# Scores by single key tiles in three PSUM banks, a fourth ring bank, and tiled products kept together

## What is computed

```python
q = _heads(h @ wq); k, v = _heads(ctx @ wk), _heads(ctx @ wv)
sim = jnp.einsum('bhnd,bhmd->bhnm', q, k) * dh ** -0.5
a = jax.nn.softmax(sim, axis=-1)                    # over 256 or 1601 keys
o = jnp.einsum('bhnm,bhmd->bhnd', a, v)
x = x + o_merged @ wo + bo
```

## Time and profile before

| | |
|---|---|
| median of 3 runs | 7120.51 us (7119.77 to 7120.83) |
| profiled execution | 7129.41 us, span 7127.6 us |
| mean granted TensorE clock | 0.956 |
| TensorE busy | 6424.0 us, 90% |
| VectorE busy | 4929.0 us, 69% |
| ScalarE busy | 3981.7 us, 56% |
| GpSimd busy | 2707.1 us, 38% |

### The profile page before, as it was taken

The page is one execution under the profiler, slowest core; times in us unless marked ns, Lnnn a source line. Parts: engine busy times, 40 slices in busy tenths (PEclk is TensorE's granted clock), DMA queues, the critical chain, the costliest instruction groups (busy, mean ns, idle before and its releaser), DMA issues.

```text
span 7127.6 us, 119830 instructions
## 1 busy us (share of the span) xinstructions
PE 6424.0 (90%) x43254; PEld 3725.9 (52%) x43254; DVE 4929.0 (69%) x9886; ACT 3981.7 (56%) x7106; POOL 2707.1 (38%) x2326
## 2 busy tenths in 40 slices
PE   6899889989889998998988999899897999989988
PEld 4555445653455544565455554556444555346644
DVE  6777666657777766665777776666577776766656
ACT  4454565655545557565654555756474445565656
POOL 2446114651144611565014551156401455116630
PEclk9999999999999999999999999999999999999999
DMA  3101011100111001111011100111001010011100
GB/s 81 33 25 26 22 27 32 28 27 18 44 32 27 25 21 31 29 30 29 12 46 31 29 24 20 33 28 30 26 16 46 25 30 24 18 35 28 29 18 11
DMA packets 347633, 204.00 MB, mean 29 GB/s; under 512 B 165006, under 2 KB 319982, under 8 KB 346927
## 3 DMA queue, kind: packets, MB, share of 16 engines
q1 hardware_dynamic: 347054, 196.34, 10.7%
HBM read 105.18 MB, written 1.05 MB: 15 GB/s over the span
## 4 chain that ended last, share of the span: by engine, by line
PE 68%; DVE 12%; ACT 9%; POOL 6%; issue 4%; SPq 1%; DVEq 0%; POOLq 0%; DMA 0%; ACTq 0%
PE ring L1309 34%; PE o_acc L1309 17%; PE scores L1309 16%; DVE max_part L2042 6%; POOL weight_sum L1271 4%; ACT qop L1593 4%; ACT probs L1719 2%; DVE region L2004 1%; DVE o_inv L2073 1%; DVE ring L2021 1%; ACT qm L1593 1%; ACT region L1593 1%; DVE ring L2018 1%; POOL qm L1290 1%; PE ring L1405 1%
## 5 line engine op out<-in xcount | busy, mean ns | idle before, releaser
L2042 DVE TENSOR_REDUCE max_part<-ring 128x1 f32<-128x400 f32 (+2 forms) x4608 | 2454.9, 578 | 829.4 <-PE ring L1309 813.8
L1719 ACT ACTIVATE probs<-scores 128x1024 f32<-128x1024 f32 (+1 forms) x2048 | 1917.6, 969 | 1231.0 <-PE scores L1309 845.3
L1271 POOL TENSOR_TENSOR weight_sum<-weight_sum,probs 128x512 f32<-128x512 f32 (+1 forms) x1408 | 1785.7, 1268 | 143.5 <-ACT probs L1719 2.4
L1309 PE MATMUL o_acc<-probs,region 128*32 128x256 f32 (+2 forms) x13312 | 1360.1, 389 | 0.0
L1271 POOL TENSOR_TENSOR weight_sum<-probs 128x512 f32<-128x512 f32 x256 | 324.8, 1269 | 2125.9 <-PE ring L1309 1794.1
L1593 ACT ACTIVATE region<-ring 64x400 f16<-64x400 f32 (+4 forms) x1744 | 815.0, 477 | 520.5 <-PE ring L1309 416.4
L1309 PEld LDWEIGHTS o_acc<-probs,region 128*32 128x32 f32 (+2 forms) x13312 | 589.0, 123 | 534.0 <-issue 317.9
L1593 ACT ACTIVATE qop<-ring 64x256 f16<-64x256 f32 (+1 forms) x1536 | 563.4, 375 | 446.9 <-DVE ring L2021 278.8
L1309 PE MATMUL scores<-qop,region 128*128 128x256 f16 (+1 forms) x3328 | 781.6, 275 | 12.6 <-ACT probs L1719 8.1
L1309 PE MATMUL ring<-nk,qm 128*128 128x400 f16 (+2 forms) x2560 | 720.6, 343 | 79.2 <-DVE max_part L2042 42.6
L1309 PE MATMUL scores<-qop,x_cop 128*128 128x256 f16 (+1 forms) x3328 | 778.0, 274 | 0.0
(11 more groups left out here) (159 smaller groups left out, 7449.6 us busy)
## 6 DMA issues: line engine op xcount, KB each, us to landing
x_cop<-region SPq DMA_DIRECT2D x256, 200.1 KB, 3.1
stage<-in_wide SPq DMA_DIRECT2D x512, 64.0 KB, 2.0
nk<-region SPq DMA_DIRECT2D x192, 100.1 KB, 2.2
stage<-in_wide SPq DMA_DIRECT2D x128, 128.0 KB, 2.6
v_stage<-in_wide SPq DMA_DIRECT2D x256, 64.0 KB, 1.8
wo_stage<-in_wide SPq DMA_DIRECT2D x32, 512.0 KB, 4.0
cop_few<-kop_few SPq DMA_DIRECT2D x256, 32.0 KB, 1.9
ff_w<-in_ff_w SPq DMA_DIRECT2D x24, 256.0 KB, 3.1
```

The costliest lines, as they stand in the source:

```text
L1271: pool.tensor_tensor(total, before, probs[0:rows_, g % PROBS, at:at + BANK], ALU.add)\
L1309: return pe.matmul(out, lhs, rhs, start=start, stop=stop, skip_group_check=True)
L1719: act.activation(to, src, ACT.Exp, scale=t.scale).then_inc(exp_done.sem, 1)
L2042: dve.tensor_reduce(dst, src, AX.X, ALU.max).then_inc(*release(one))
```

## The change

Scores, exponentials and probabilities go by single key tiles: a chunk is one tile, `scores` has three banks for three chunks, `probs` eight slots of half the size. The bank that this frees goes to the ring, now four. Value products, the GpSimd sums and the release of probability slots still go by pairs of tiles (`chunks_of`). The due times of the scores are spread evenly over a unit's time. The planner's `run` remembers whether TensorE's last part used column tiles (`in_tiles`: value products and `sum`); a part of the other kind counts as due `STAY = 1.0` later, and 0.1 longer. The planned costs of scores, exponentials and value products are restated. The diff without its context lines:

```diff
@@ -23,7 +23,9 @@
-RING, SLOTS, PROBS = 3, 2, 4
+RING, SLOTS, PROBS = 4, 3, 8
+STAY = 1.0
@@ -40,7 +42,7 @@
-        self.chunks = self.pairs * self.halves
+        self.chunks = self.kt * self.halves
@@ -89,6 +91,10 @@
+    def chunks_of(self, pair):
+        return range(2 * pair * self.halves, min(2 * pair + 2, self.kt) * self.halves)
@@ -236,8 +242,8 @@
-                half = prev.t.halves == 2 and prev.t.cross and cb % 2 == 0
-                at = values_at[prev.n, cb // prev.t.halves] - 0.001 - half * 0.5 * prev.t.time / prev.t.pairs
+                t = prev.t
+                at = values_at[prev.n, 0] - 0.001 + (cb / t.chunks) * t.time * (t.cross or 0.5)
@@ -246,8 +252,11 @@
+            at = max(at, done.get("scores", at) + 0.0001)
+            if c == 0:
+                scores_at[un.n] = at
...
-            scored[un.n] = at
+            scored[un.n] = done["scores"] = at
@@ -360,6 +369,11 @@
+def in_tiles(what):
+    return what[0] == "values" or what[0] == "job" and UNITS[what[1]].t.jobs[what[2]][0] == "sum"
@@ -381,9 +395,10 @@
-        out = [("PE", ("values", un.n, c // un.t.halves))]
+        pair = c // un.t.halves // 2
+        out = [("PE", ("values", un.n, pair))]
...
-            out.append(("POOL", ("values", un.n, c)))
+            out.append(("POOL", ("values", un.n, pair)))
@@ -567,7 +582,6 @@
-        pair = c // t.halves
@@ -575,18 +589,17 @@
-        tiles = len(t.tiles(pair))
-        self.part("PE", "scores", due, one, (0.45 if t.wide else 0.23) * tiles, deps, 0.2)
+        self.part("PE", "scores", due, one, 0.44 if t.wide else 0.22, deps, 0.2)
...
-        self.part("ACT", "exp", due, one, 1.02 if tiles == 2 else 0.6, deps)
+        self.part("ACT", "exp", due, one, 0.58, deps)
...
-        deps = [("ACT", ("scores", un.chunk + pair * t.halves + k)) for k in range(t.halves)]
+        deps = [("ACT", ("scores", un.chunk + c)) for c in t.chunks_of(pair)]
@@ -597,12 +610,11 @@
-        self.part("PE", "values", due, one, 0.53 * tiles, deps, 0.25)
+        self.part("PE", "values", due, one, 0.43 * tiles, deps, 0.25)
...
-            deps = [("ACT", ("scores", un.chunk + pair))]
...
-                deps.append(("PE", ("job", old.n, old.t.sum_job)))
+                deps = [*deps[:t.chunks_of(0)[-1] + 1], ("PE", ("job", old.n, old.t.sum_job))]
@@ -650,7 +662,7 @@
-        events, now, left = [], 0.0, len(self.parts)
+        events, now, left, tiled = [], 0.0, len(self.parts), False
@@ -660,6 +672,8 @@
+                    if e == "PE" and in_tiles(what) != tiled:
+                        due = due[0] + STAY, due[1]
@@ -672,6 +686,9 @@
+                if e == "PE":
+                    dur += 0.1 * (in_tiles(what) != tiled)
+                    tiled = in_tiles(what)
@@ -836,7 +853,7 @@
-        probs = sb("probs", [P, PROBS, 2 * BANK])
+        probs = sb("probs", [P, PROBS, BANK])
@@ -868,7 +885,7 @@
-        scores = psum("scores", [P, 2 * SLOTS, BANK])
+        scores = psum("scores", [P, SLOTS, BANK])
@@ -1252,8 +1269,7 @@
-                    g = un.chunk + pair
-                    pool.wait_ge(exp_done.sem, exp_done.at(n, pair + 1))
+                    pool.wait_ge(exp_done.sem, exp_done.at(n, t.chunks_of(pair)[-1] + 1))
@@ -1261,14 +1277,13 @@
-                        at = (k % 2) * BANK
...
-                        before = probs[0:rows_, g % PROBS, 0:BANK] if k == 1 else total
+                        before = probs[0:rows_, un.chunk % PROBS, :] if k == 1 else total
...
-                        pool.tensor_tensor(total, before, probs[0:rows_, g % PROBS, at:at + BANK], ALU.add)\
+                        pool.tensor_tensor(total, before, probs[0:rows_, (un.chunk + k) % PROBS, :], ALU.add)\
@@ -1516,7 +1531,7 @@
-                    pair, half = c // t.halves, c % t.halves
+                    k, half = c // t.halves, c % t.halves
@@ -1526,18 +1541,16 @@
-                    first = 2 * (g % SLOTS)
-                    for k in t.tiles(pair):
-                        r = t.rows(k)
-                        if t.wide:
-                            out = scores[0:r, first + k % 2, :]
-                            for h in range(2):
-                                mm(out[:, h * N:(h + 1) * N], kop_of(un)[:, h, k * P:k * P + r], qop[:, z, h, :], True, False)
-                                last = mm(out[:, h * N:(h + 1) * N], cop_of(un)[:, h, k * P:k * P + r], qop[:, z, 2 + h, :],
-                                          False, True)
-                        else:
-                            last = mm(scores[0:r, first + k % 2, :], nk[:, un.narrow_at % NK_SLOTS, k * P:k * P + r],
-                                      qm[:, un.narrow_at % QM_SLOTS, 2 * half:2 * half + 2, :], True, True)
+                    r = t.rows(k)
+                    out = scores[0:r, g % SLOTS, :]
+                    if t.wide:
+                        for h in range(2):
+                            mm(out[:, h * N:(h + 1) * N], kop_of(un)[:, h, k * P:k * P + r], qop[:, z, h, :], True, False)
+                            last = mm(out[:, h * N:(h + 1) * N], cop_of(un)[:, h, k * P:k * P + r], qop[:, z, 2 + h, :],
+                                      False, True)
+                    else:
+                        last = mm(out, nk[:, un.narrow_at % NK_SLOTS, k * P:k * P + r],
+                                  qm[:, un.narrow_at % QM_SLOTS, 2 * half:2 * half + 2, :], True, True)
@@ -1555,14 +1568,13 @@
-                    pe.wait_ge(exp_done.sem, exp_done.at(n, (pair + 1) * t.halves))
+                    pe.wait_ge(exp_done.sem, exp_done.at(n, t.chunks_of(pair)[-1] + 1))
...
-                        r, at = t.rows(k), k % 2
+                        r = t.rows(k)
...
-                            g = un.chunk + pair * t.halves + h // 2
-                            slot = g % PROBS
-                            w = probs[0:r, slot, at * BANK + (h % 2) * N:at * BANK + (h % 2 + 1) * N]
+                            g = un.chunk + k * t.halves + h // 2
+                            w = probs[0:r, g % PROBS, (h % 2) * N:(h % 2 + 1) * N]
@@ -1701,21 +1713,15 @@
-                    pair = c // t.halves
...
-                        act.wait_ge(av_done.sem, av_done.at(old.n, co // old.t.halves + 1))
+                        pair = co // old.t.halves // 2
+                        act.wait_ge(av_done.sem, av_done.at(old.n, pair + 1))
...
-                            act.wait_ge(weight_step.sem, weight_step.at(old.n, old.t.adds(co)))
-                    to = probs[:, g % PROBS, :].rearrange("p (k n) -> p k n", k=2)
-                    src = scores[:, 2 * (g % SLOTS):2 * (g % SLOTS) + 2, :]
-                    last_tile = t.tiles(pair)[-1]
-                    r = t.rows(last_tile)
-                    if len(t.tiles(pair)) == 2:
-                        to, src = to[0:r, :, :], src[0:r, :, :]
-                    else:
-                        to, src = to[0:r, 0, :], src[0:r, 0, :]
+                            act.wait_ge(weight_step.sem, weight_step.at(old.n, old.t.adds(pair)))
+                    r = t.rows(c // t.halves)
+                    to, src = probs[0:r, g % PROBS, :], scores[0:r, g % SLOTS, :]
```

## The result

The changed kernel takes 6657.7 us against 7120.7: ratio 0.9347, 95% interval 0.9331 to 0.9363, 463 us less. The forecast was 6870 us in a range from 6700 to 7110: the right direction, and 1.85 times the gain.

The account below looks back on a forecast made before the run. TensorE and VectorE were taken to wait for each other across three ring banks. From the profiled 7129.4 us, -270 (ring), -20 (visits) and +40 (scores) gave 6879, less 8.9 to the median: 6870 us, range 6700 to 7110.

Parts of the forecast that it names:

- What bounds the kernel: Whole kernel: TensorE (90% busy) and VectorE (69%) wait for each other; three ring banks between them are too short a queue.
- The ring term: TensorE's ring products: a fourth bank takes 0.5 us off each of 540 waits, -270 us.
- the bounds of 156 and 415: Ring waits: 156 us saved if the bank helps once per run of two waits, 415 us if every wait goes.
- The upper bound of 831 us: Ring bank: adds the weight loads' waits for maxima and `qop`, 433.7 + 68.8 us, partly covered by TensorE's running products.
- Kept together: TensorE's column-tile products grouped by the planner: 100 visits fewer at 0.19 us each, -20 us; bounds 0 and -128 us.
- due times 3 and 4 apart: Cross units' value products: due 4.0 (wide) or 3.0 (narrow) apart, so STAY's 1.0 was not expected to join them.
- the sums ride along: Cross units: the sum of weights comes within 1.0 of the next unit's first value product, so it can share its visit.
- Single tiles: Scores and ScalarE's exponentials by one tile: 285 us more ScalarE work, mostly hidden, +40 us; bounds -169 and +285.
- VectorE did not pace the ring: Rival that VectorE paces the ring: the bank gives about 40 us, 7100 us in all, 7120 as likely; chance 0.12.
- The score rival: Three single-tile score banks cover ScalarE too little: 0.43 us per cross pair, priced at 900 pairs, 7215 us; chance 0.14.
- Joined value pairs: Rival that readiness lets value pairs follow each other: 672 visits fewer instead of 100, 6762 us; chance 0.12.
- The order does not change: Rival: visits stay near 1536, 20 us less gain, 6890 us; inside the forecast's range, no chance of its own.

Follow-up runs that it names:

- experiment 5: Changed kernel with four ring banks, planner keeping one always spare, so the order is that of three ring and three score banks: 6903.5 us, ratio 0.9701.
- experiment 3: Kernel before the change with only the planner's rule on column tiles (STAY = 1.0, 0.1 per switch, value products at 0.43 a tile): 7109.6 us, ratio 0.9986.
- experiment 1: Changed kernel with three ring banks instead of four, three score banks, one PSUM bank left empty: 7083.0 us, ratio 0.9947.
- experiment 6: Changed kernel with two score banks instead of three, one PSUM bank unused, and an added wait between VectorE's maxima: 6939.1 us, ratio 0.9751.

## Why the prediction was too small

**What bounds the kernel: right.** TensorE and VectorE each stood idle for the other, with three banks between them. A bank in that queue, with its order, carries 425 of 463 us.

**The ring term: the step that failed.** It took the waits of the order as it stood and asked what a free bank takes off each: "I take 0.5 us from each of the 540", 270 us. Two things in this step were wrong. What the sum did not hold at all is that the order is made anew with a bank more: 246 us. The planner's condition "if a bank is free" was in the code and had been read; I treated it as a limit on waits, not on what the planner can choose. And depth at a fixed order gave 180 us (experiment 5), inside the bounds of 156 and 415 but below my choice. Nor did it come off the listed waits, whose sum over all kinds stayed (590.3 and 586.7 us). It came as busy time, 161 us, and beside the weight loads' waits, which I had named and then left out of the choice. I had let the term be bounded by 415 us, and the measured 425 lies above that. The upper bound of 831 us written beside it leaves out its own tails; with them it is 415 + 433.7 + 68.8 = 918 us. The ring term is 155 of the 212 us that the forecast missed; the other 57 are the next two terms.

**The clock: no term.** Up to 134 of the 472 us between the profiles come as a higher granted clock, spread over the terms above.

**Kept together: wrong in sign, small in size.** I expected 100 visits fewer; there are 38 more. The argument that due times 3 and 4 apart keep value pairs from joining does not hold: 85 pairs were joined already before, 65 are in the changed kernel, and STAY = 1.0 in the kernel before raised 85 to 157. Nor did the sums ride along: 113 visits hold a sum and no value product, where 95 did before. That a ring product is more often ready with four banks, and so interrupts, I had not seen. The price of 0.19 us stands in the rows; what a visit is worth in time was 0.06 us in experiment 3 and 0.18 and 0.29 in two steps of STAY.

**Single tiles: too dear.** Scores at +40 and visits at -20 made +20 us; experiment 1 has both, with the new due times and costs, at -35. ScalarE's busy time rose by 169 us, not 285. How much the finer pieces gained and how much the planner's costs did was not separated.

**The rivals.** VectorE did not pace the ring. The score rival did not come, but experiment 6 found its place one bank lower, and at 281 us. Joined value pairs are fewer in the changed kernel than before; at STAY = 3.0 there are 340. "The order does not change" was nearly true of the number of visits and false of everything else, and there lay the 246 us that the sum did not hold.

## What to carry to other kernels

When two engines each wait for the other across a short queue, one more buffer can be worth more than the listed waits of the trace, if the order is planned from the number of buffers: a little over half of the gain here came from the order. Look at busy time too: short stops and a lower clock hide in it. Size such a change in two parts, depth at the fixed order and the freedom of the planner, and let a spare buffer tell them apart. Small waits on a buffer do not say that one can be taken away. In the changed kernel the waits for a score bank are 29.0 us, and taking one of the three away cost 281 us.

## What the runs showed of the hardware

A pair's exponential of 1.023 us became two of 0.599, by which ScalarE's exponentials should take 1792 x 0.175 = 314 us more. The page's busy time for them rose from 1917.6 to 2104.7 us, 187 us, because the ends of exponentials that follow each other directly overlap in it: 3840 x 0.599 = 2300 us of durations lie in 2104.7 us, and 2048 x 0.969 = 1985 lay in 1917.6. For this split the sum of single durations overstates what the engine loses.

A visit to the column tiles has a price of 0.19 us in TensorE's starts. Before and after the change alike, a full product follows 1.01 us after the first of eight `o_acc` products, and a tiled one 0.91 us after it. After a one-product maximum `o_acc` starts 0.26 to 0.27 us later, and scores 0.17 to 0.18.
